# Routed attention: the query product cut by query tile and issued inside the loop over heads

## What is computed

```python
def gqa(x, wq, wk, wv, wo, n_kv):
    B, S, _ = x.shape
    groups = N_HEADS // n_kv
    q = (x @ wq).reshape(B, S, N_HEADS, D_K).transpose(0, 2, 1, 3)
    k = (x @ wk).reshape(B, S, n_kv, D_K).transpose(0, 2, 1, 3)
    v = (x @ wv).reshape(B, S, n_kv, D_K).transpose(0, 2, 1, 3)
    k = jnp.repeat(k, groups, axis=1)
    v = jnp.repeat(v, groups, axis=1)
    scores = jnp.einsum('bhqd,bhkd->bhqk', q, k) / jnp.sqrt(jnp.float32(D_K))
    attn = jax.nn.softmax(scores, axis=-1)
    out = jnp.einsum('bhqk,bhkd->bhqd', attn, v)
    out = out.transpose(0, 2, 1, 3).reshape(B, S, D_MODEL)
    return out @ wo
```

## Time and profile before

| what | value |
|---|---|
| time before, median of 3 runs | 5624.57 us (5622.45 to 5626.36) |
| time of the profiled execution | 5618.81 us |
| its span in the trace | 5617.0 us |
| TensorE busy, whole span | 4898.8 us (87%) |
| VectorE busy, whole span | 2794.0 us (50%) |
| ScalarE busy, whole span | 1428.1 us (25%) |
| first k product of the stage starts | 5372.9 us |
| mean granted clock, whole span | 0.961 of full speed |

### The profile page before, as it was taken

The page is one execution under the profiler, slowest core; times in us unless marked ns, Lnnn a source line. Parts: engine busy times, 40 slices in busy tenths (PEclk is TensorE's granted clock), DMA queues, the critical chain, the costliest instruction groups (busy, mean ns, idle before and its releaser), DMA issues. The chain is left out here.

```text
span 5617.0 us, 281252 instructions
## 1 busy us (share of the span) xinstructions
PE 4898.8 (87%) x116024; PEld 3206.5 (57%) x117274; DVE 2794.0 (50%) x11344; ACT 1428.1 (25%) x4662; POOL 633.4 (11%) x1073
## 2 busy tenths in 40 slices
PE   8899686999898988888888888888888888868789
PEld 6644343444565446666666666666666666644556
DVE  4500344232554665555555555555555555554524
ACT  0000000012232353333333333333333333322313
POOL 0000283000563110000000000000000000010200
PEclk9999897999999999999999999999999999989878
DMA  0000111167443850000000000000000000001000
GB/s 11 15 30 15 28 41 34 45 219 256 137 120 100 296 146 22 12 11 11 11 12 11 11 11 11 12 11 11 11 12 11 11 11 11 8 27 41 16 32 10
DMA packets 153467, 259.51 MB, mean 46 GB/s; under 512 B 47554, under 2 KB 81480, under 8 KB 149037
## 3 DMA queue, kind: packets, MB, share of 16 engines
q1 hardware_dynamic: 98344, 176.13, 9.4%
q0 software_dynamic: 55040, 82.30, 5.1%
HBM read 172.87 MB, written 85.14 MB: 46 GB/s over the span
## 5 line engine op out<-in xcount | busy, mean ns | idle before, releaser
L1558 PE MATMUL bank<-lstm_w,step_h_parts 128*32 128x128 f16 x94848 | 1558.0, 220 | 101.6 <-issue 5.5
L1558 PEld LDWEIGHTS bank<-lstm_w,step_h_parts 128*32 128x32 f16 x94848 | 1341.1, 97 | 451.8 <-issue 300.3
L1630 DVE TRANSPOSE_TENSOR_REDUCE step_summed<-bank 128x4 f32 (+1 forms) x2500 | 792.0, 317 | 1061.1 <-PE bank L1558 895.7
L1553 PE MATMUL bank<-step_xg,step_rows 128*128 (+1 forms) x1252 | 476.0, 381 | 277.9 <-issue 258.2
L1526 ACT ACTIVATE step_act_out<-step_summed,lstm_inv_scale 128x4 f32<-128x4 f32 x625 | 185.8, 297 | 1707.9 <-DVE step_summed L1630 1707.9
L1514 POOL COPY xnT<-step_state 128x4 f32 (+1 forms) x625 | 116.4, 186 | 2743.9 <-DVE step_state L1655 2743.9
L1179 PE MATMUL bank<-sum_parts,sum_hot 125*125 125x512 f16 x1600 | 348.0, 381 | 6.6 <-DVE sum_parts L1138 6.6
L1179 PEld LDWEIGHTS bank<-sum_parts,sum_hot 125*125 125x125 f16 x1600 | 219.8, 137 | 135.2 <-DVE sum_parts L1138 7.7
L1429 PE MATMUL bank<-xg_w,xnT 128*125 128x512 f32 x640 | 277.1, 596 | 6.6 <-DMA xg_w<-in_c_w_ih 6.6
L538 POOL DMA_INDIRECT gcn_rows<-gcn_h_rows,gcn_idx x160 | 202.0, 1262 | 698.6 <-issue 698.3
L1553 PEld LDWEIGHTS bank<-step_xg,step_rows 128*128 128x128 bf16 x2500 | 142.7, 98 | 210.1 <-issue 131.1
(11 more groups left out here) (364 smaller groups left out, 6289.8 us busy)
## 6 DMA issues: line engine op xcount, KB each, us to landing
rel_h<-rel_h_sb SPq DMA_DIRECT2D x39, 1024.0 KB, 6.4
lstm_xg<-cnt POOLq DMA_DIRECT2D x80, 375.0 KB, 4.3
step_xg<-lstm_xg SPq DMA_DIRECT2D x375, 80.0 KB, 2.4
xg_w<-in_c_w_ih SPq DMA_DIRECT2D x16, 1024.0 KB
lstm_w<-in_c_w_hh SPq DMA_DIRECT2D x16, 1024.0 KB, 12.6
cheb_w<-in_L_gnn_weight SPq DMA_DIRECT2D x8, 1024.0 KB
choose_we<-in_L_ffn_experts SPq DMA_DIRECT2D x8, 1024.0 KB
rel_bases<-in_L_gnn_bases SPq DMA_DIRECT2D x8, 1024.0 KB, 11.1
```

The costliest lines, as they stand in the source:

```text
L1553: return nc.tensor.matmul(bank[:], rows[:, p, :], xg[:, at, :], start=True, stop=stop)
L1558: last = nc.tensor.matmul(bank[32 * q:32 * q + 32, 128 * s:128 * s + 128], h_parts[:, c, :], w[:, s, c, q, a, 128 * p:128 * p + 128], star ...
L1630: nc.vector.tensor_reduce(summed[:, 4 * p:4 * p + 4], bank[:, bass.ds(s * 128, 128)].rearrange("p (b r) -> p b r", r=32), X_AXIS, ALU.add, ...
```

## The change

The query product leaves the loop that it shared with k. It is cut by row tile: `queries(m)` makes all 512 features of 125 rows, as four blocks of 125 columns side by side in bank 7, and ScalarE copies the whole tile out in one instruction (`keep_q`). `queries(0)` comes behind k, and the others inside the loop, one tile ahead, at the first head of the tile before. The scores of heads 0 and 1 move ahead of the value products; these go through banks 4, 5, 6, 4, 6, and VectorE's copies of them move behind the row maxima of heads 0 and 1. The waits follow: `scores` at head 0 of a tile waits for the copy of its queries, `queries(3)` and `queries(4)` wait until the product in bank 7 was added to x, `turn_out` waits for the copy of the queries that used bank 7 before it. The wait for wo moves from ahead of the loop to its ninth index. SP's program is the same.

```diff
+    V_BANK = (4, 5, 6, 4, 6)
...
-            for n in range(2 * KC):
-                dve.wait_ge(qk_done, n + 1)
-                dst = (kT, qT)[n // KC]
-                nc.vector.tensor_copy(dst[:, n % KC, 500:N], B.bank[2 * (n % 2) + 1][:, 0:R]).then_inc(qk_tail_kept, 1)
-            for m in range(NT):
-                dve.wait_ge(v_done, m + 1)
-                nc.vector.tensor_copy(v[:, m, :, 0:DK], B.bank[4 + m % 4][0:R, :].rearrange("p (h d) -> p h d", h=AH)
-                                      ).then_inc(v_kept, 1)
+            for n in range(KC):
+                dve.wait_ge(k_done, n + 1)
+                nc.vector.tensor_copy(kT[:, n, 500:N], B.bank[2 * (n % 2) + 1][:, 0:R]).then_inc(k_tail_kept, 1)
...
+            def keep_v(m):
+                dve.wait_ge(v_done, m + 1)
+                nc.vector.tensor_copy(v[:, m, :, 0:DK], B.bank[V_BANK[m]][0:R, :].rearrange("p (h d) -> p h d", h=AH)
+                                      ).then_inc(v_kept, 1)
+
             row_max(0)
             row_max(1)
+            for m in range(NT):
+                keep_v(m)
             for i in range(M + 1):
...
-            for n in range(2 * KC):
-                act.wait_ge(qk_done, n + 1)
-                dst = (kT, qT)[n // KC]
-                nc.scalar.copy(dst[:, n % KC, 0:500], B.bank[2 * (n % 2)][:, 0:500]).then_inc(qk_kept, 1)
+            for n in range(KC):
+                act.wait_ge(k_done, n + 1)
+                nc.scalar.copy(kT[:, n, 0:500], B.bank[2 * (n % 2)][:, 0:500]).then_inc(k_kept, 1)
+
+            def keep_q(m):
+                act.wait_ge(q_done, m + 1)
+                nc.scalar.copy(qT[:, :, m * R:(m + 1) * R], B.bank[7][:, 0:500].rearrange("p (c r) -> p c r", c=KC)
+                               ).then_inc(q_kept, 1)
...
+            keep_q(0)
             expo(0)
             expo(1)
             for i in range(M):
                 keep_turned(i)
                 if i + 2 < M:
                     expo(i + 2)
+                if i % AH == 0 and i // AH + 1 < NT:
+                    keep_q(i // AH + 1)
...
+            def queries(m):
+                if m >= 3:
+                    pe.wait_ge(added, m - 2)
+                for n in range(KC):
+                    for c in range(KC):
+                        last = nc.tensor.matmul(B.bank[7][:, n * R:(n + 1) * R], wq[:, c, n * 128:(n + 1) * 128],
+                                                xnT[:, c, m * R:(m + 1) * R], start=(c == 0), stop=(c == KC - 1))
+                last.then_inc(q_done, 1)
+
+            def values(m):
+                if m == 3:
+                    pe.wait_ge(v_kept, 2)
+                if m == 4:
+                    pe.wait_ge(v_kept, 4)
                 for c in range(KC):
-                    last = nc.tensor.matmul(B.bank[4 + m % 4][0:R, :], xnT[:, c, m * R:(m + 1) * R], wv[:, c, :],
+                    last = nc.tensor.matmul(B.bank[V_BANK[m]][0:R, :], xnT[:, c, m * R:(m + 1) * R], wv[:, c, :],
                                             start=(c == 0), stop=(c == KC - 1))
                 last.then_inc(v_done, 1)
...
+                if hd == 0:
+                    pe.wait_ge(q_kept, m + 1)
                 q = qT[lo:lo + DK, hd // 2, m * R:(m + 1) * R]
...
             def turn_out(m):
                 pe.wait_ge(o_kept, AH * (m + 1))
-                if m >= 1:
+                if m + 2 < NT:
+                    pe.wait_ge(q_kept, m + 3)
+                elif m >= 1:
                     pe.wait_ge(added, m)
...
+            pe.wait_ge(wq_loaded, 16)
+            queries(0)
+            pe.wait_ge(k_kept, KC)
+            pe.wait_ge(k_tail_kept, KC)
             scores(0)
             scores(1)
-            pe.wait_ge(v_kept, NT + 1)
-            pe.wait_ge(wo_loaded, 16)
+            pe.wait_ge(wv_loaded, 16)
+            for m in range(NT):
+                values(m)
+            pe.wait_ge(v_kept, NT)
             for i in range(M + 1):
                 if i < M:
                     turn(i)
...
                     sum_values(i - 1)
+                if i < M and i % AH == 0 and i // AH + 1 < NT:
+                    queries(i // AH + 1)
+                if i == AH:
+                    pe.wait_ge(wo_loaded, 16)
                 if i >= AH and i % AH == 2:
                     turn_out(i // AH - 1)
```

More of the change, by code:

```diff
@@ L2109, in routed_attention @@
     (r_loaded, mean_step, hidden_done, hidden_ready, logit_done, pick_step, exp_done, picked, wq_loaded, wk_loaded,
-     wv_loaded, wo_loaded, qk_done, qk_kept, qk_tail_kept, v_done, v_kept, s_done, max_step, max_ready, exp_ready,
+     wv_loaded, wo_loaded, k_done, k_kept, k_tail_kept, q_done, q_kept, v_done, v_kept, s_done, max_step, max_ready, exp_ready,
      p_turned, pT_kept_a, pT_kept_v, o_done, inv_ready, o_kept, o_turned, oT_kept, out_done, added,
@@ L2113, in routed_attention @@
          "r_loaded mean_step hidden_done hidden_ready logit_done pick_step exp_done picked wq_loaded wk_loaded "
-         "wv_loaded wo_loaded qk_done qk_kept qk_tail_kept v_done v_kept s_done max_step max_ready exp_ready "
+         "wv_loaded wo_loaded k_done k_kept k_tail_kept q_done q_kept v_done v_kept s_done max_step max_ready exp_ready "
          "p_turned pT_kept_a pT_kept_v o_done inv_ready o_kept o_turned oT_kept out_done added "
@@ L2305, in _ @@
             pe.wait_ge(wk_loaded, 16)
[L2306 to L2309, removed]
+            for n in range(KC):
                 if n >= 2:
-                    pe.wait_ge(qk_kept, n - 1)
-                    pe.wait_ge(qk_tail_kept, n - 1)
+                    pe.wait_ge(k_kept, n - 1)
+                    pe.wait_ge(k_tail_kept, n - 1)
                 b = 2 * (n % 2)
                 for c in range(KC):
-                    wt = (wk, wq)[n // KC][:, c, c2 * 128:(c2 + 1) * 128]
+                    wt = wk[:, c, n * 128:(n + 1) * 128]
                     nc.tensor.matmul(B.bank[b][:, 0:500], wt, xnT[:, c, 0:500], start=(c == 0), stop=(c == KC - 1))
@@ L2318, in _ @@
                                             stop=(c == KC - 1))
[L2319 to L2323, removed]
+                last.then_inc(k_done, 1)
+            def queries(m):
+                if m >= 3:
+                    pe.wait_ge(added, m - 2)
+                for n in range(KC):
+                    for c in range(KC):
[7 more added lines that the diff above has]
+                    pe.wait_ge(v_kept, 4)
                 for c in range(KC):
-                    last = nc.tensor.matmul(B.bank[4 + m % 4][0:R, :], xnT[:, c, m * R:(m + 1) * R], wv[:, c, :],
+                    last = nc.tensor.matmul(B.bank[V_BANK[m]][0:R, :], xnT[:, c, m * R:(m + 1) * R], wv[:, c, :],
                                             start=(c == 0), stop=(c == KC - 1))
                 last.then_inc(v_done, 1)
-            pe.wait_ge(qk_kept, 2 * KC)
-            pe.wait_ge(qk_tail_kept, 2 * KC)
             def scores(i):
@@ L2354, in sum_values @@
                 pe.wait_ge(pT_kept_v, i + 1)
+                if i == 0:
+                    pe.wait_ge(v_kept, NT + 1)
                 if i >= 1:
```

## The result

| | before | changed |
|---|---|---|
| median of four runs each | 5624.39 us (5622.45 to 5626.36) | 5588.73 us (5587.51 to 5589.27) |
| profiled execution | 5618.81 us | 5587.51 us |
| its span | 5617.0 us | 5585.7 us |
| the stage: first k product to the end of the span | 5372.9 to 5617.0 = 244.1 us | 5378.8 to 5585.7 = 206.9 us |

The ratio is 0.9936 (95% interval 0.992 to 0.9951), 35.7 us less by the medians, where 36.6 less was forecast (5588). The two profiled executions differ by 31.3 us only: all that lies ahead of the stage took 5.8 us longer in the second. That difference builds up in stages that the change doesn't touch (their first products start 1.6 us later at 275.6 us and 5.0 us later at 644.1 us already), so I compare the stage by its own length, 244.1 against 206.9: 37.2 us less.

A forecast was written before the change was run, and what follows sets the result against it. TensorE's own work bounds the stage, and its granted clock sets the time. −35.6 − 2.3 + 0.6 + 0.7 = −36.6 us takes the profiled 5618.81 to 5582.2, or 5588 as a median; range 5581 to 5602.

The forecast's parts named there:

- The clock term: Tile loop, turn(0) to turn(13): 78.29 us would become 42.66 if the clock stays at 2.4 GHz, −35.6 us.
- The pause: TensorE's 2.26 us idle time before turn(0), to be covered by the value products moved there: −2.3 us.
- The query product: Split by row tile into 160 passes of 0.11 us, 17.6 us against 17.01: +0.6 us.
- the row with 0.190 us of the weight load: Upper bound for query passes: if loads stop overlapping, each costs 0.190 us, 30.4 us in all, +13.4 us.
- The new pause: Before scores(0), TensorE waits for ScalarE's copy of queries(0): +0.7 us.
- The end: End of the stage, with its clock fall and last projection: little change, 2.5 us either way.
- Loads: Rival: weight loads bound the query passes; net −23.8 us, 5601 us, chance 0.05.
- The loop doesn't take the clock down by itself: Denies the rival that the tile loop lowers the clock: 5612 us (chance 0.04) or 5627 us (chance 0.05).
- The slower rival: TensorE stalls on bank 7 after each query product and the clock falls each time: +29, 5654 us, chance 0.04.
- The rule of the Trainium skill: Brief idling between matmul groups while cycling PSUM banks can swing the clock; by it, bank 7 would give 5654 us.
- the clock would hold: Granted clock stays 1.00 through the loop, argued from 80 us of the same loop and the graph-attention loop.
- The 2.4 us for a rise: Price in the rivals for raising a low clock by dense products: half of 4.7 us until the rise.

The follow-up runs named there:

- e3: Kernel before, order kept, with three extra 128x512 matmuls, never read, filling the 2.26 us idle time after scores 0 and 1: 5592.10 us, ratio 0.9935.
- e1: Kernel before with only the order changed, scores 0 and 1 ahead of the value products, query product left whole: 5590.78 us, ratio 0.9933.
- e4: Kernel before, pause included, with six extra 128x512 matmuls, never read, in the slow loop after the value sums of head index 1: 5602.48 us.
- e6: Changed kernel with the fourth value product made to wait for four unread ScalarE copies, a 2.32 us pause among dense products: 5593.74 us.
- e9: Changed kernel with values(0) before scores(0), seven extra matmuls ahead of k and three at the stage's end: 5582.67 us, ratio 0.9923 to the kernel before.
- e5: Kernel before with one extra 128x512 matmul after scores 0 and 1, leaving 1.11 us of idle time: 5625.26 us, ratio 0.9985.
- e2: Changed kernel with the value products back ahead of scores 0 and 1, so the 2.26 us pause returns; query products stay in the loop: 5591.13 us.

## Why the prediction was right

**The clock term** (−35.6) was the whole matter and came out as reckoned. The new loop takes 49.9 us from `turn(0)` to `turn(13)`; less `queries(1)` and `queries(2)`, 3.67 (5423.22 to 5426.89 in the timeline) and 3.62, that is 42.6 us, where 42.66 was built up from heads of the fast part: −35.7. (The fast part is the 27 heads from `turn(13)` on, somewhat less than the four tiles that the prediction speaks of.) e3 shows that the idle time caused the slow stretch, e1 that closing it is enough, e4 that the low clock is a state which the loop is left in and not one that it makes, and e6 that a pause of this length brings a fall between dense products too.

**The pause** (−2.3) is gone, as the timeline shows, and the copies of v behind the row maxima delayed nobody.

**The query product** (+0.6) was sized a little low: 3.59 + 3.77 + 3 x 3.62 = 18.2 us against 17.01, +1.2. A pass takes 0.114 us in a row of 32, where the pairs showed 0.11; the row with 0.190 us of the weight load was far off, loads do overlap. **The new pause** (+0.7) measured 0.76 us. **The end**, put at ±2.5 us, gave −1.1: from `turn(13)` to the end of the span it is 114.5 us less 7.2 for two query products, 107.3 against 108.4, 0.6 of it from the last projection. The prediction had no reason for a gain there (over the runs that projection took 5.10 to 6.75 us with the same pauses ahead of it), so it is luck that it makes up for the dearer query product. Together −35.7 − 2.3 + 1.2 + 0.8 − 1.1 = −37.1, within 0.1 of the stage's 244.1 − 206.9.

**The rivals.** Loads don't bound the passes. The loop doesn't take the clock down by itself. The slower rival needed idle TensorE behind the query products, and there is none: `turn` follows `queries` in every tile, at 1.00. The rule of the Trainium skill that stood beside it ("TensorE: Matmul & The Clock Gate", section "A second HAM failure mode: psum-queue depth-cycling") says of a kernel that cycles through banks that short idling between its groups of matmuls made the clock swing. Bank 7 with its two users shows no idle time and no swing here, but the end of the stage, with pauses of 0.58 to 0.67 us, did fall until e9 filled them.

**What was thin in it.** I argued that the clock would hold because another loop idles 1.02 us a head at 1.00 and the new pause is shorter. e5 fell with 1.11 us. The forecast stood on the safe side by less than its text suggests: the new pause of 0.76 us held, but 0.35 us more, at another place, fell in eight of ten executions. The 2.4 us for a rise, half of the 4.7 seen at the projection, is not a fixed price either: in e4 the rise came after 2.4 us and in e2 the fall cost 1.6.

**What stays open.** Which pause is just too long at a given place: 0.76 us ahead of two score tiles and the dense value products held, and so did 1.02 us in each head of the graph-attention loop; 1.11 us ahead of transposes fell in eight of ten executions, and three pauses of at most 0.67 us fell at the end of the stage. What differs between those executions was not tried.

## What to carry to other kernels

When one loop runs at two speeds in one trace, look at the granted clock before anything else, and then at what TensorE did in the few microseconds ahead of the fall; a short wait can cost many times its own length if only narrow products follow it (here 2.26 us cost 35.6 more). Order independent dense work into such a wait, or, if none is left, fill it with products that nobody reads, and leave some dense work in a long narrow loop, so that a fall which does happen is soon over. TensorE at 100% busy says nothing of this: the slow 70 us were as busy as the fast ones.

## What the runs showed of the hardware that I had not expected

The granted clock of a long run of matmuls depended on how it was entered: the same unbroken tile loop stayed at 0.50 for 70 us and, after a projection, at 1.00 for 80 us in one trace (e5), each at 100% busy; with the query products in it, it stayed at 1.00 for 140 us (e2). Idle time of 2.32 us in the midst of 128x512 products brought a fall (e6), and idle time of 1.11 us ahead of transposes did in eight of ten executions (e5). Six products that compute nothing, 6.4 us of them, made the kernel 24 to 26 us faster (e4).
